# Group norms, FFN weights and weighted values of a convolution and attention block put in another order

## The reference

```python
x = x + depthwise_conv(group_norm(x, 32 groups), 11x11 kernels)
t = tokens(x)                                   # 16 x 256 x 96
t = t + proj(causal_attention(layer_norm(t)))   # 6 heads of 16, rotary q and k
h = quantise(layer_norm(t) @ sign(W1 - group mean) + b1)
t = t + quantise(gelu(h) @ sign(W2 - group mean) + b2)
```

## Time and profile before

| what | value |
|---|---|
| median of 3 runs | 262.8 us (262.58 to 263.31) |
| the profiled execution's own time | 261.93 us |
| its span, first to last instruction | 260.0 us |
| PE busy | 223.0 us, 86% |
| PE weight loads (PEld) | 169.9 us, 65% |
| DVE busy | 204.9 us, 79% |
| ACT busy | 134.8 us, 52% |
| POOL busy | 113.4 us, 44% |
| mean granted TensorE clock | 0.938 |

### The profile page before, as it was taken

How to read it: one execution, slowest core, us unless ns; L and a number is a source line. 1 busy time by engine, 2 the same in 40 slices (tenths; PEclk the granted TensorE clock), 3 DMA queues, 4 the chain that set the end, 5 groups by cost and what they waited for, 6 DMA issues and landing times.

```text
span 260.0 us, 5342 instructions
## 1 busy us (share of the span) xinstructions
PE 223.0 (86%) x1794; PEld 169.9 (65%) x1794; DVE 204.9 (79%) x530; ACT 134.8 (52%) x308; POOL 113.4 (44%) x143
## 2 busy tenths in 40 slices
PE   6479598998999968589999889898987989999990
PEld 6369587978988946457767777677754635545550
DVE  3857859999999776979898788884858568898965
ACT  1341417766664554447876668576754214426250
POOL 1201154655665563437787444895463405010101
PEclk9759999999999997979999999999996599999996
DMA  4999000579999900040344405300000000101103
GB/s 111 246 333 150 1 0 0 95 123 120 120 122 191 147 2 2 1 94 20 91 80 90 86 12 109 77 5 3 0 3 1 0 0 3 45 1 45 45 3 106
DMA packets 22828, 17.43 MB, mean 67 GB/s; under 512 B 3089, under 2 KB 22162, under 8 KB 22802
## 3 DMA queue, kind: packets, MB, share of 16 engines
q1 hardware_dynamic: 21200, 15.81, 33.5%
q10 hardware_dynamic: 1602, 1.29, 2.1%
HBM read 6.03 MB, written 1.57 MB: 29 GB/s over the span
## 4 chain that ended last, share of the span: by engine, by line
PE 50%; DVE 12%; issue 5%; ACT 2%; DVEq 0%
PE bank L1620 8%; PE bank L1569 8%; PE bank L1737 7%; PE bank L1509 5%; DVE nmax L1076 5%; PE bank L1540 3%; PE bank L1429 2%; PE bank L1407 2%; PE bank L1521 2%; PE bank L1588 2%; PE bank L1604 1%; PE bank L1542 1%; PE bank L1758 1%; PE bank L1554 1%; PE bank L1580 1%
## 5 line engine op out<-in xcount | busy, mean ns | idle before, releaser
L1076 DVE TENSOR_REDUCE nmax<-bank 128x3 f32<-128x384 f32 x64 | 45.4, 750 | 12.3 <-PE bank L1509 12.1
L734 ACT ACTIVATE pt_ring<-bank 128x384 f32<-128x384 f32 x96 | 42.1, 493 | 15.0 <-PE bank L1542 14.3
L1407 PE MATMUL bank<-xs_ring,toep 128*128 128x192 f32 x256 | 47.3, 334 | 1.2 <-DVE xs_ring L944 1.2
L532 POOL TENSOR_SCALAR_AFFINE_SELECT pt_ring<-pt_ring 128x512 f32<-128x512 f32 x48 | 31.2, 658 | 37.3 <-ACT pt_ring L734 37.3
L1407 PEld LDWEIGHTS bank<-xs_ring,toep 128*128 128x128 f32 x256 | 43.2, 195 | 3.3 <-issue 2.1
L1509 PE MATMUL bank<-stack 128*128 128x128 bf16 (+1 forms) x288 | 23.1, 225 | 5.7 <-DVE nmax L1076 3.7
L489 POOL TENSOR_TENSOR parts<-rest_ring,parts 96x512 bf16<-96x512 f32 x16 | 20.8, 1302 | 16.3 <-ACT parts L666 16.3
L1620 PE MATMUL bank<-parts,w_b 97*128 97x256 f32 (+1 forms) x60 | 25.4, 539 | 0.0
L1509 PEld LDWEIGHTS bank<-stack 128*128 128x128 bf16 (+1 forms) x288 | 18.0, 100 | 11.2 <-issue 7.0
L1737 PE MATMUL bank<-parts,w_b 128*96 128x512 f32 (+1 forms) x60 | 23.1, 492 | 1.5 <-issue 1.3
L1540 PE MATMUL bank<-stack 97*128 97x256 bf16 x96 | 23.3, 279 | 0.2 <-ACT pt_ring L734 0.2
(11 more groups left out here) (145 smaller groups left out, 434.6 us busy)
## 6 DMA issues: line engine op xcount, KB each, us to landing
stack<-parts SPq DMA_DIRECT2D x96, 96.0 KB, 3.7
tok<-in_x_tok SPq DMA_DIRECT2D x4, 384.0 KB, 12.1
stack<-in_const SPq DMA_DIRECT2D x1, 1152.0 KB, 18.7
out<-xs_ring SPq DMA_DIRECT2D x4, 288.0 KB, 2.6
stack<-in_x ACTq DMA_DIRECT2D x2, 384.0 KB, 8.6
stack<-in_const SPq DMA_DIRECT2D x1, 576.0 KB, 7.3
stack<-nmax_t SPq DMA_DIRECT2D x32, 1.5 KB
stack<-in_x SPq DMA_DIRECT2D x2, 192.0 KB, 4.5
```

The costliest lines, as they stand in the source:

```text
L532: nc.gpsimd.affine_select(out=v, in_=v, compare_op=ALU.is_ge, fill=0.0, base=0, pattern=[[0, 2], [0, 2], [1, P]], channel_multiplier=-1).t ...
L734: nc.scalar.activation(pt_ring[:, b % 2, h, :], bank[:, 3 + h % 2, 0:T + P], ACT.Exp, scale=float(HD) ** -0.5).then_inc(s_exp, 1)
L1076: last = nc.vector.tensor_reduce(nmax[:, b % 2, k:k + 3], bank[:, 0:3, first:first + (t + 1) * P], op=ALU.max, axis=AX.X, negate=True)
L1407: last = nc.tensor.matmul(dst, w, xs_ring[:, s, p, k].rearrange("p b c -> p (b c)"), start=(part == 0 and p == 0), stop=(part == 1 and p = ...
```

## The change

- `PV_ORDER` becomes two lists, heads 0 to 3 (8 products) and heads 4 and 5 (6 products). `weighted_values` is called once for each, with the second group of scores between the two. The transposition of queries and keys in steps 1 to 3 moves behind `transpose_o`.
- The FFN weights' sums are made by DVE behind the statistics of images 4 to 7, added by PE behind the second mean sums, and the means by DVE behind the second variance. GpSimd centres and zeroes the weights in its step 1. The projection weights' load counts on a semaphore of its own.
- The last group norm (k = 2) is spread over step 2 of PE, DVE and GpSimd, its sums go to bank 7, and ACT normalises pair 4 behind `ln_out`. PE's `project_qkv` of the first images goes from step 1 to step 2.
- `warm_up` is called with 14, 4, 12 and 5 instead of 9, 1 and 4.

```diff
@@ -60,9 +60,9 @@
 MASK_SIZES = [5] * 3 + [4] * 28
 SHIFT = 0
 
-PV_ORDER = ([(h, h, 0, P, T, 0) for h in range(4)] + [(h, h, 1, 0, P, P) for h in range(4)]
-            + [(0, 4, 0, T, P, 2 * P), (1, 5, 0, T, P, 2 * P), (2, 4, 0, P, P, 2 * P), (3, 5, 0, P, P, 2 * P)]
-            + [(0, 4, 1, 0, P, 2 * P), (1, 5, 1, 0, P, 2 * P)])
+PV_ORDER = ([(h, h, 0, P, T, 0) for h in range(4)] + [(h, h, 1, 0, P, P) for h in range(4)],
+            [(0, 4, 0, T, P, 2 * P), (1, 5, 0, T, P, 2 * P), (2, 4, 0, P, P, 2 * P), (3, 5, 0, P, P, 2 * P),
+             (0, 4, 1, 0, P, 2 * P), (1, 5, 1, 0, P, 2 * P)])
...
@@ -345,7 +346,7 @@
-            return bank[0:C, 4, first:first + n] if k < 2 else bank[0:C, 6, 3 * P + first:3 * P + first + n]
+            return bank[0:C, 4, first:first + n] if k < 2 else bank[0:C, 7, 3 * P + first:3 * P + first + n]
@@ -497,13 +498,30 @@
...
+            def centre_weights():
+
+                pool.wait_ge(s_wmean, 1)
+                v1 = w1_b[0:C, 0:QGROUPS * W1_ROWS].rearrange("c (g r) -> c g r", g=QGROUPS)
+                nc.gpsimd.tensor_tensor(v1, v1, w_mean[0:C, 0, :].unsqueeze(2).broadcast_to([C, QGROUPS, W1_ROWS]),
+                                        ALU.subtract).then_inc(s_wcen, 1)
+                for k in range(HC):
+                    v2 = w2_b[:, k, 0:QGROUPS * W2_ROWS].rearrange("p (g r) -> p g r", g=QGROUPS)
+                    last = nc.gpsimd.tensor_tensor(
+                        v2, v2, w_mean[:, 1, :].unsqueeze(2).broadcast_to([P, QGROUPS, W2_ROWS]), ALU.subtract)
+                last.then_inc(s_wcen, 1)
+                nc.gpsimd.memset(w1_b[0:C, QGROUPS * W1_ROWS:HID], 0.0)
+                nc.gpsimd.memset(w2_b[:, :, QGROUPS * W2_ROWS:C], 0.0).then_inc(s_wready, 1)
+
             def step_a(i, n0):
                 if n0 >= 1:
                     ln_rstds(i, n0 - 1)
                 if n0 == 1:
+                    centre_weights()
+                if n0 >= 2:
+                    sines(i, n0 - 2, 0)
+                if n0 == 2:
                     gn_rstds(2)
                 if n0 >= 2:
-                    sines(i, n0 - 2, 0)
                     sines(i, n0 - 2, 1)
                 if n0 >= 3:
@@ -691,14 +709,15 @@
-                if n0 == 2:
-                    act.wait_ge(s_gshift, 3)
-                if n0 + 2 < PAIRS and n0 >= 1:
+                if n0 + 2 < PAIRS and n0 != 2:
                     normalise(i, n0 + 2)
                 if n0 >= 2:
                     first_parts(i, n0 - 2, 0)
                 if n0 >= 1:
                     ln_out(i, n0 - 1)
+                if n0 == 2:
+                    act.wait_ge(s_gshift, 3)
+                    normalise(i, n0 + 2)
@@ -944,6 +963,21 @@
 
+            def weight_sums():
+
+                dve.wait_ge(s_weights, 16 * 4)
+                nc.vector.tensor_reduce(w_sum[0:C, 0, :], w1_b[0:C, 0:QGROUPS * W1_ROWS].rearrange(
+                    "c (g r) -> c g r", g=QGROUPS), op=ALU.add, axis=AX.X)
+                nc.vector.tensor_reduce(w_sum[:, 1, :], w2_b[:, :, 0:QGROUPS * W2_ROWS].rearrange(
+                    "p k (g r) -> p g k r", g=QGROUPS), op=ALU.add, axis=AX.XY).then_inc(s_wsum, 1)
+
+            def weight_means():
+
+                dve.wait_ge(s_wps, 1)
+                nc.vector.tensor_scalar(w_mean[0:C, 0, :], bank[0:C, 7, 0:QGROUPS], 1.0 / (W1_ROWS * C), None, ALU.mult)
+                nc.vector.tensor_scalar(w_mean[:, 1, :], bank[:, 7, QGROUPS:2 * QGROUPS], 1.0 / (W2_ROWS * HID), None,
+                                        ALU.mult).then_inc(s_wmean, 1)
+
             cone(0)
             gn_shifts(0)
             cone(1)
@@ -953,9 +987,11 @@
             weigh(0, 0)
             gn_stats(range(4, 8))
             gn_channels(1)
+            weight_sums()
             gn_means(1)
             weigh(0, 1)
             gn_vars(1)
+            weight_means()
             gn_stats(range(8, 12))
@@ -1011,39 +1047,26 @@
-            def weight_means():
...
-            def centre_w1():
...
-            def centre_w2():
...
             def step_a(i, n0):
                 if n0 >= 1:
                     add_conv(i, n0 - 1)
                     ln_stats(i, n0 - 1)
+                if n0 == 2:
+                    gn_means(2)
                 if n0 >= 2:
                     cosines(i, n0 - 2, 0)
                 if n0 >= 3:
                     second_parts(i, n0 - 3, 1)
                 if n0 + 1 < PAIRS:
                     weigh(i, n0 + 1)
+                if n0 == 2:
+                    gn_vars(2)
                 if n0 >= 2:
                     rotate(i, n0 - 2, 0)
                     cosines(i, n0 - 2, 1)
+                if n0 == 2:
+                    gn_shifts(2)
+                if n0 >= 2:
                     rotate(i, n0 - 2, 1)
                     second_parts(i, n0 - 2, 0)
 
@@ -1051,20 +1074,7 @@
             step_a(0, 1)
             gn_stats(range(12, B))
             gn_channels(2)
-            gn_means(2)
-            gn_vars(2)
-            gn_shifts(2)
             run(step_a, 2, PAIRS - 1)
...
-            def weight_sums(k):
...
@@ -1138,23 +1148,12 @@
                     cosines(0, PAIRS - 1, n - 1)
                 if n >= 3:
                     add_attention(n - 3)
-                if n == 6:
-                    weight_means()
                 if n + 3 < B:
                     maxima(n + 3, 1)
                 if n == 0:
                     rotate(0, PAIRS - 2, 1)
                 if n in (1, 2):
                     rotate(0, PAIRS - 1, n - 1)
-                if n in (4, 5):
-                    weight_sums(n - 4)
-                if n == 6:
-                    centre_w1()
-                if n == 7:
-                    centre_w2()
-                if n == 8:
-                    nc.vector.memset(w1_b[0:C, QGROUPS * W1_ROWS:HID], 0.0)
-                    nc.vector.memset(w2_b[:, :, QGROUPS * W2_ROWS:C], 0.0).then_inc(s_wready, 1)
                 if n == 9:
                     second_stats(0)
 
@@ -1378,12 +1377,12 @@
                 for k in range(count):
                     nc.tensor.matmul(bank[:, 7, 0:P], ident[:], ident[:], start=True, stop=True)
             pe.wait_ge(s_ident, 1)
-            warm_up(9)
+            warm_up(14)
             pe.wait_ge(s_same, 16)
             gn_mean_sums(0)
-            warm_up(1)
+            warm_up(4)
             gn_var_sums(0)
-            warm_up(4)
+            warm_up(12)
 
             def transpose_pair(i, n0):
@@ -1413,6 +1412,10 @@
                 b = 2 * (n0 + 2 * i) + u
                 pe.wait_ge(s_rope, b + 1)
                 wait(pe, s_rest, b)
+                if b == 0:
+                    pe.wait_ge(s_gvar, 3)
+                if b == 0:
+                    pe.wait_ge(s_wmean, 1)
@@ -1441,15 +1444,16 @@
-                pe.wait_ge(s_wsum, 2)
-                nc.tensor.matmul(bank[0:C, 6, 0:QGROUPS], ones[0:C, 0:C], w_sum[0:C, 0, :], start=True, stop=True)
-                nc.tensor.matmul(bank[:, 6, QGROUPS:2 * QGROUPS], ones[:], w_sum[:, 1, :], start=True,
+                pe.wait_ge(s_wsum, 1)
+                nc.tensor.matmul(bank[0:C, 7, 0:QGROUPS], ones[0:C, 0:C], w_sum[0:C, 0, :], start=True, stop=True)
+                nc.tensor.matmul(bank[:, 7, QGROUPS:2 * QGROUPS], ones[:], w_sum[:, 1, :], start=True,
                                  stop=True).then_inc(s_wps, 1)
 
...
             pe.wait_ge(s_wa, 16)
             pe.wait_ge(s_centre, 1)
             nc.tensor.matmul(bank[0:C, 6, 0:3 * C], centre[:], wa[:], start=True, stop=True).then_inc(s_wac, 1)
+            warm_up(5)
             pe.wait_ge(s_toep, POINTS)
@@ -1457,28 +1461,29 @@
                 pe.wait_ge(s_xs, j + 1)
                 wait(pe, s_tok, j - 1)
                 convolve(i, n0, 0, 0)
+                if n0 == 2:
+                    gn_mean_sums(2)
+                    pe.wait_ge(s_wacopy, 1)
+                    project_qkv(i, 0, 0)
                 if n0 >= 2:
                     transpose_pair(i, n0 + 1)
-                if n0 >= 2:
+                if n0 >= 3:
                     project_qkv(i, n0 - 2, 1)
                 convolve(i, n0, 0, 1)
                 if n0 == 1:
                     transpose_pair(i, n0 + 1)
+                if n0 == 2:
+                    gn_var_sums(2)
+                    project_qkv(i, 0, 1)
                 convolve(i, n0, 1, 0)
-                if n0 == 1:
-                    pe.wait_ge(s_wacopy, 1)
-                    gn_mean_sums(2)
                 if n0 >= 2:
                     transpose_qk(i, n0 - 2, 0)
-                if n0 >= 1:
                     transpose_ln(i, n0 - 1)
                 convolve(i, n0, 1, 1).then_inc(s_cv, 1)
+                if n0 == 1:
+                    transpose_ln(i, n0 - 1)
                 if n0 >= 2:
                     transpose_qk(i, n0 - 2, 1)
-                if n0 == 1:
-                    gn_var_sums(2)
-                    pe.wait_ge(s_gvar, 3)
-                if n0 >= 1:
```

(35 more changed lines are left out.)

23 lines of the change are left out of this document (2 added, 21 removed).

## The result

The changed kernel takes **253.66 us** (four runs, 253.2 to 254.39) against 262.69 (261.3 to 263.31) of the kernel before: ratio 0.9729, interval 0.9668 to 0.979. Predicted was 255.1, within 251 to 259. The profiled executions took 253.84 and 261.93 us, 8.1 apart, and the sum of the prediction was 7.7. The sum came out right, but not its terms, as five marks in the two traces show. Executions of one and the same kernel differ by some us with the mean clock that TensorE was granted (down to 0.925 in slow ones); medians are over all of them, ratios over the fast ones, and each trace is of one. W2 is the start of VectorE's weighting of pair 2, S3 step 3's first addition, A1 and A12 VectorE's second maxima in attention steps 1 and 12, FFN the first product of the FFN's second layer.

What follows compares the result with a forecast made beforehand. No engine is idle enough to be free, so the order of waits on TensorE and VectorE decides. 1.2 + 2.8 + 2.7 + 0.5 + 0.5 = 7.7 us off 262.8 gives 255.1 us, range 251 to 259.

Steps and rivals of the forecast that it cites:

- Opening, 1.2 us: 0 to 27 us: more idle products raise TensorE's clock early; weighting of pair 2 starts at 25.95 instead of 27.11.
- The weight products: Opening: TensorE's two products for the FFN weights' sums, four records, cost 0.5 us on its path.
- Last group norm, 2.8: Convolution step 2: its work fills VectorE's waits; pair 2's weighting to step 3's first addition takes 13.2 instead of 16.04 us.
- Centring, 2.5 us charged at nothing: Weight centring on GpSimd takes 2.5 us (bounds 1.1 and 5), about 27 us, where GpSimd stands 5.21 us.
- FFN weights, 2.7: Attention steps 4 to 8: without weight work, the six periods from step 3 to 9 take 29.8 us, gain 2.7.
- The split, 0.5 + 0.5: Attention: second scores start 0.52 us earlier, switches cost 0.19 a step; net 0.5 us, plus 0.5 in step 1.
- rival (c): Attention: the split costs what it gives, 0.35 us a step for switches; 257.1 us, chance 0.16.
- the two steps with rotations: Attention steps with the moved transposition of queries and keys: 5.66 us become 5.40, gaining 0.52 together.
- Step 9 to 10: Attention period with the second layer norm's statistics, bound by VectorE, 6.00 us: gains 0.52 from the split.
- The 0.5 us of step 1: Attention step 1: VectorE idles 1.47 us before its second maxima; the split gives 0.8 less 0.3 of switches.
- The clock, charged at nothing: Behind the opening, the sum of terms held no gain or loss from changed half-clock stretches.
- Rival (b): A kinder clock: the fall from 197 to 208 us stays away, worth some 4 us; 251 us, chance 0.14.

Runs made afterwards that it cites:

- e1: The kernel before with only the idle products at the beginning changed (14, 4, 12 and 5 for 9, 1, 4 and none): 261.87 us.
- e3: The changed kernel with the FFN weights prepared late, on VectorE in attention steps 4 to 8, as in the kernel before: 254.30 us.
- e5: The changed kernel with the FFN weights prepared late and without the split: 257.67 us.
- e12: The kernel before with all idle products (beginning, transition, end of the attention) and none of the new orders: 254.93 us.
- e4: The changed kernel with the last group norm in one piece between steps 1 and 2, as in the kernel before: 261.61 us.
- e11: e10 without the split, the transposition of steps 1 to 3 in its old place: 248.62 us, ratio 0.9517.
- e10: The changed kernel with idle products in the transition (5, 6 and 4) and 7 in the wait near 189.5 us: 251.02 us.
- e6: The changed kernel with 5, 6 and 4 idle products in three waits of TensorE in the transition from convolution to attention: 251.20 us.
- e9: The changed kernel once more, unaltered, run on one chip together with e10 to e12: 254.89 us.
- e7: The kernel before with 7 idle products in TensorE's wait for the tokens at 197.8 us: 262.06 us, ratio 0.9958.

## Why the prediction was right, and where it was not

**Opening, 1.2 us: right in kind.** Transposes at 13.27, the sums hidden in the stall, W2 1.52 us earlier. The term was small by 0.3, which no run can attribute: W2 lies between 24.96 and 25.59 in the eight traces with this opening and the weights in it. The weight products cost 0.4 (W2 is at 25.32 in the mean of these eight, at 24.94 in that of e1, e3, e5 and e12, which have the idle products only); 0.5 was predicted.

**Last group norm, 2.8: 2.2.** The order works as said. What was mis-sized is the power: 2.66 us for 1.63, 1.03 more. The chain ahead of it took 8.80 us (8.95 + 0.1 predicted), and from its end to the last rotation it was 0.98 (1.08 + 0.1), which leaves the 0.6 us. The shift grew too, 0.95 for 0.16, but costs nothing: the sine beside it, which the last rotation needs as well, ends at the same time (38.00 and 38.03). The new wait of VectorE is 1.53 us, 1.3 predicted. In e4, where VectorE stands during the power, it takes 1.63 us again. The trace before showed the same thing from the other side, in a line that the prediction did not use: the second cosine of step 2, beside the sine of GpSimd at 40.17, where a cosine in the trace after, with no sine beside it, takes 0.54:

```profile
40.31 1.36 DVE L967 TENSOR_TENSOR rc_ring<-qk_ring,cst 128x384 f32<-128x384 f32 x1
```

The Trainium skill ("SBUF — State Buffer", Terms) says that VectorE and GpSimd share a pair of ports which one holds for a whole instruction while the other stands. The traces agree: the shift begins 0.07 us behind the sine and ends 0.03 behind it, and the power is longer by 1.03 us where VectorE's rotation and cosine last 1.15 us into it, though which of them held the ports when is not shown. The tile sizes are as before.

**Centring, 2.5 us charged at nothing: right**, 1.8 us in GpSimd's pause.

**FFN weights, 2.7: right only for a kernel without the split.** e12 to e11 gives 2.73 us from A1 to FFN, which is the term. But in the changed kernel the same work done late costs 0.50 (e3, 88.98 against 88.48), and its gain in the opening's two products is 0.4. This is the step that failed: the prediction added two gains that draw on one reserve. The traces show the reserve. The weight work stands between VectorE's second maxima and its reciprocal. Without the split VectorE has no wait there, so the normalisation comes later by the whole of it, and PE, which needs the normalised values ahead of `transpose_max`, stands. The centring of W2 in the kernel before, on VectorE and behind it on PE:

```profile
151.03 0.85 DVE L1030 TENSOR_TENSOR w_b<-w_b,w_mean 128x95 f32<-128x95 f32 x3
152.62 0.27 PE L1554 MATMUL bank<-ident,nmax 128*12 128x128 f32 x1 [0.69 <-DVE o_norm L1109]
```

With the split the maxima begin earlier against the rest of PE's step, and VectorE has its 0.38 us of idle time ahead of the reciprocal. The same work in e3, with no wait for normalised values on PE in this step:

```profile
147.29 0.58 DVE L989 TENSOR_TENSOR w_b<-w_b,w_mean 128x95 f32<-128x95 f32 x3
147.79 0.23 DVE L1123 RECIPROCAL rsum<-bank 128x12 f32<-128x12 f32 x1
```

Of e3's five steps with weight work, four take 4.98 to 5.02 us, as plain ones do; only the one in which VectorE and PE wait for each other over the sums takes 5.64.

**The split, 0.5 + 0.5: wrong in sign.** The switches cost 0.19 us a step, exactly the figure, and a plain step is 4.98 us (4.95 predicted) instead of 4.89. The Trainium skill's rule on weight loads ("TensorE: Matmul & The Clock Gate", Part 3), by which rival (c) was the likelier, is not contradicted, but the 0.35 us a step of that rival did not come. What failed are the gains. From A1 to A12 (e10 against e11, in us) the two steps with rotations gain 0.1 together, not 0.52: they take 5.54 and 5.65 where 5.40 was predicted. Step 3 to 4 loses 0.32, not 0.06. Step 9 to 10 gains 0.37, not 0.52. With 0.09 lost in each of seven plain steps it comes to a loss of 0.48, where a gain of 0.5 was predicted. The 0.5 us of step 1 did not come: S3 to A1 takes 70.55 us in e6 and 70.54 in e11. And one cost is missing from the sum: in step 12, the last with such scores, the second lot of weighted values stands behind the scores, and nothing at the end of the stage gets earlier by the earlier maxima. A12 to FFN is 0.65 us longer with the split (30.68 in e9 and e10, 30.03 in e11). TensorE in this step, in e10:

```profile
167.59 0.69 PE L1519 MATMUL bank<-stack 128*128 128x128 bf16 x9
168.77 0.28 PE L1550 MATMUL bank<-stack 97*128 97x256 bf16 x1
171.11 0.27 PE L1564 MATMUL bank<-ident,nmax 128*12 128x128 f32 x1 [0.58 <-DVE o_norm L1119]
```

and in e11:

```profile
165.82 0.69 PE L1519 MATMUL bank<-stack 128*128 128x128 bf16 x9
166.34 0.27 PE L1550 MATMUL bank<-stack 97*128 97x256 bf16 x1
168.70 0.27 PE L1564 MATMUL bank<-ident,nmax 128*12 128x128 f32 x1 [0.73 <-DVE o_norm L1119]
```

From the scores to the next product it is 1.18 us with the split and 0.52 without. The wait for the normalised values, by which the expectation of e11 explained the loss, is no shorter without the split: 0.73 us against 0.58. With late weights the split gains 0.64 (A1 to FFN, e12 89.62, e3 88.98), with early ones it costs 1.13 (e10, e11).

**The clock, charged at nothing: 3.8 us for, 1.0 against.** Rival (b), given 0.14, came in part. The fall at 197 is gone, which is worth 33.88 - 30.05 = 3.83 us (the kernel before against e7 and e12). In the transition the half-clock stretches cost 74.10 - 70.55 = 3.55 us in the changed kernel (against e6), 73.26 - 70.72 = 2.54 before (against e12). So 1.96 + 3.07 - 0.84 = 4.2 us of the attention and its two ends met a prediction of 3.7, by other causes: 2.8 of the 4.2 are the clock's. Of the predicted 7.7 us of orders and opening some 5.1 came (1.5 + 2.2 + 0.2 + 1.2), and the clock gave the rest. The total was right in part by luck. With the idle products in both kernels, the new orders are worth 3.8 us at FFN (e12 202.76, e10 198.99), and 6.2 without the split (e11, 196.57).

**Open.** Behind the opening, the falls begin close to waits of TensorE of 1 to 3 us, within them or less than 0.9 us off: at 29.2 (e12; wait of 2.66 up to 28.77), at 39.7 (e10; 2.10 up to 38.98), at 189.4 (e6; 1.70 up to 189.51), at 197.1 before (1.70 up to 197.83). Filling such waits took the falls away there in e6, e7, e10, e11 and e12. But the changed kernel has 1.69 up to 193.72 and no fall, and a wait of 2.1 us that ends between 38.98 and 39.61 is in nine traces, of which only e9 and e10 have a fall there. So a wait is not enough for one; that waits bring the falls is argued and not shown, and what decides between executions was not settled. Added products also shift everything behind them in time, and no run separates the two. Idle products in the wait of 2.09 us that the changed order has at 39.6 were not tried.

## What to carry to other kernels

Price an edit against the kernel with all other edits in it: two that relieve the same wait give one gain, and the second may only cost. Before reordering work, read the granted clock beside TensorE's waits, and try idle products into a free bank there: 15 of them in three waits of 1.0 to 1.7 us gave 3.8 us at A1, more than any new order here. A scheduling gain that is measured as the start of something inside a step counts only once the end of the last step has moved too.
